# Keys and values by batch around the second batch's transposes, and the second heads of the first chunk half a granule later

## The reference

```
x = x + fake_quant(layernorm(x)) @ fake_quant(ctx)          # ctx: 2 x 2048 x 2048
h = layernorm(x)
q = h @ Wq                     # 2048 x 2048, 32 heads of 64
k, v = split(h @ Wkv)          # 2048 x 128: one key and one value head for all
p = softmax(causal(q k^T / 8 + alibi))
x = x + (p v) @ Wo             # 2048 x 2048
x = x + layernorm(x) @ dequant4(qweight, qzeros, scales) + bias
```

## Time and profile before

| | |
|---|---|
| median of 3 runs | 400.56 us (400.42 to 400.67) |
| profiled execution | 400.76 us |
| its span, first to last instruction | 398.9 us |
| granted TensorE clock, mean | 0.983 |
| PE busy | 353.4 us, 89% of the span |
| DVE busy | 328.7 us, 82% |
| ACT busy | 221.5 us, 56% |
| POOL busy | 29.7 us, 7% |
| DMA | 77.37 MB, mean 194 GB/s |

### The profile page before, as it was taken

The page is one execution under the profiler, slowest core; times in us unless marked ns, Lnnn a source line. Parts: engine busy times, 40 slices in busy tenths (PEclk is TensorE's granted clock), DMA queues, the critical chain, the costliest instruction groups (busy, mean ns, idle before and its releaser), DMA issues.

```text
span 398.9 us, 5679 instructions
## 1 busy us (share of the span) xinstructions
PE 353.4 (89%) x2321; PEld 262.9 (66%) x2326; DVE 328.7 (82%) x333; ACT 221.5 (56%) x316; POOL 29.7 (7%) x69
## 2 busy tenths in 40 slices
PE   0076867788799998999999999999999999999996
PEld 0022222325688786878877888888888788888884
DVE  1689889886877898785989968898988999999924
ACT  1788988998524873655855680743824923333100
POOL 6000000006590000000002000000000000000000
PEclk9999986999999999999999999999999999999999
DMA  8999999999063476496448733876000020000006
GB/s 327 426 429 434 428 422 432 430 395 379 6 218 128 182 194 197 140 214 209 159 159 248 218 108 115 305 273 257 3 0 1 0 107 0 2 0 0 2 0 210
DMA packets 21958, 77.37 MB, mean 194 GB/s; under 512 B 1354, under 2 KB 1402, under 8 KB 18810
## 3 DMA queue, kind: packets, MB, share of 16 engines
q1 hardware_dynamic: 21924, 77.01, 52.9%
q10 hardware_dynamic: 8, 0.00, 0.0%
HBM read 74.91 MB, written 2.10 MB: 193 GB/s over the span
## 4 chain that ended last, share of the span: by engine, by line
PE 69%; DMA 13%; DVE 9%; ACT 6%; issue 2%; ACTq 0%
PE bank L1186 21%; PE bank L1049 12%; PE bank L1050 12%; PE bank L1051 12%; DMA ctx_more<-in_ctx 12%; ACT q L462 5%; PE bank L1062 2%; PE bank L1131 2%; PE bank L1150 2%; DVE w_lo L652 2%; PE bank L1072 2%; DMA prm_row<-in_L_xattn_x_zp 1%; PE bank L1042 1%; DVE stats L622 1%; ACT a L467 1%
## 5 line engine op out<-in xcount | busy, mean ns | idle before, releaser
L486 ACT ACTIVATE w_hi<-raw 128x2048 fp32r<-128x2048 f32 x29 | 55.2, 1912 | 44.6 <-DMA raw<-in_L_attn_Wo 23.0
L652 DVE TENSOR_TENSOR w_lo<-raw,w_hi 128x2048 fp32r<-128x2048 f32 x27 | 62.4, 2321 | 13.2 <-ACT w_hi L486 13.2
L1186 PE MATMUL bank<-w_hi,hd 128*128 128x512 f32 x208 | 53.1, 391 | 0.1
L1010 PE MATMUL bank<-q,at 128*128 128x512 bf16 x123 | 38.0, 436 | 15.9 <-DVE q L708 14.7
L1186 PEld LDWEIGHTS bank<-w_hi,hd 128*128 128x128 f32 x208 | 38.8, 188 | 8.4 <-issue 0.5
L708 DVE TENSOR_SCALAR q<-q 128x2048 bf16<-128x2048 uint8 x32 | 38.4, 1218 | 4.9 <-PE bank L1017 3.0
L1049 PE MATMUL bank<-w_hi,hd 128*128 128x512 f32 x104 | 40.7, 391 | 0.0
L1050 PE MATMUL bank<-w_lo,hd 128*128 128x512 f32 x104 | 40.5, 389 | 0.0
L1051 PE MATMUL bank<-w_hi,hd 128*128 128x512 f32 x104 | 40.5, 389 | 0.0
L1049 PE MATMUL bank<-w_hi,xt 128*128 128x512 f32 x96 | 38.9, 405 | 0.0
L1050 PE MATMUL bank<-w_lo,xt 128*128 128x512 f32 x96 | 37.5, 390 | 0.0
(11 more groups left out here) (160 smaller groups left out, 618.0 us busy)
## 6 DMA issues: line engine op xcount, KB each, us to landing
raw<-in_ctx SPq DMA_DIRECT2D x8, 2048.0 KB, 15.4
raw<-in_L_attn_Wq SPq DMA_DIRECT2D x16, 1024.0 KB, 5.5
ctx_more<-in_ctx SPq DMA_DIRECT2D x7, 2048.0 KB, 16.2
raw<-in_L_attn_Wo SPq DMA_DIRECT2D x13, 1024.0 KB, 5.2
raw_fifth<-in_L_attn_Wo SPq DMA_DIRECT2D x3, 1024.0 KB, 5.1
resid<-in_x SPq DMA_DIRECT2D x2, 1024.0 KB, 12.7
ctx_more<-in_ctx SPq DMA_DIRECT2D x2, 1024.0 KB, 15.4
scale<-in_L_ffn_scales SPq DMA_DIRECT2D x16, 128.0 KB, 6.4
```

What stands on the lines that cost most here:

```text
L486: nc.scalar.activation(hi_slots[s], raw_slots[s], ACT.Copy).then_inc(w_hi_set, 1)
L652: nc.vector.tensor_tensor(lo_slots[s], raw_slots[s], hi_slots[s].bitcast(F32), ALU.subtract).then_inc(w_lo_set, 1)
L1010: mm(bank[:, 4 * b + n, :], at[:, k, b * P:(b + 1) * P], q16[:, i % 2, n * CH:(n + 1) * CH], start=start, stop=False)
L1186: return mm(bank[:, 4 * b + n, :], left[:, j, b * P:(b + 1) * P], right[slot_of(W_F + j)][:, n * CH:(n + 1) * CH], start=part == 0 and j = ...
```

## The change

On ACT the high part of the key and value weight is made ahead of `upper(1, g)`. On PE `keys_values` is replaced by `kv_by_upper(b)` (16 matmuls of 256 columns: both parts of x of one batch, with the high part of the weight) and `kv_by_lower()` (16 of 256 columns: high part of x of both batches, with the low part). `kv_by_upper(0)` stands right behind `transposes(1)`, the other two where `keys_values` stood. `q_by_lower(1, 0)` moves from behind the transposes to ahead of them. In the first turn of the loop (n = 1) `attend(ub)` moves behind `q_granule(w + 3, 1)`; in the others it stays.

```diff
             sqrt_of(3)
-            for g in range(4):
-                upper(1, g)
             act.wait_ge(wkv_loaded, 16)
             act.wait_ge(at_done, B)
             nc.scalar.activation(kv_hi_t, kv_raw[:], ACT.Copy).then_inc(kv_hi_set, 1)
+            for g in range(4):
+                upper(1, g)
...
-            def keys_values():
-
+            def kv_by_upper(b):
+
+                pe.wait_ge(kv_hi_set, 1)
+                pe.wait_ge(lo_out, 4 * (b + 1))
+                pe.wait_ge(resid1, B * NCH)
+                m = slice(b * P, (b + 1) * P)
+                for k in range(KT):
+                    mm(bank[:, KV_BANK, :].rearrange("p (x m) -> p x m", x=2)[:, :, m], kv_hi_t[:, k * P:(k + 1) * P],
+                       xt[:, :, k, m], start=b == 0 and k == 0, stop=False)
+
+            def kv_by_lower():
                 pe.wait_ge(kv_lo_set, 1)
-                pe.wait_ge(lo_out, 8)
-                pe.wait_ge(resid1, B * NCH)
                 for k in range(KT):
-                    c = slice(k * P, (k + 1) * P)
-                    if k > 0:
-                        mm(bank[:, KV_BANK, 0:B * P], kv_lo_t[:, c], xt_hi[:, k, :], start=False, stop=False)
-                    ins = mm(bank[:, KV_BANK, :], kv_hi_t[:, c], xt[:, :, k, :], start=k == 0, stop=k == KT - 1)
-                    if k == 0:
-                        mm(bank[:, KV_BANK, 0:B * P], kv_lo_t[:, c], xt_hi[:, k, :], start=False, stop=False)
+                    ins = mm(bank[:, KV_BANK, 0:B * P], kv_lo_t[:, k * P:(k + 1) * P], xt_hi[:, k, :],
+                             start=False, stop=k == KT - 1)
                 ins.then_inc(kv_done, 1)
...
             q_by_upper(3, 0)
+            q_by_lower(1, 0)
             transposes(1)
-            q_by_lower(1, 0)
+            kv_by_upper(0)
             for w in range(2):
                 q_by_upper(w, 1)
                 q_by_lower(w, 1)
...
             q_by_upper(3, 1)
-            keys_values()
+            kv_by_upper(1)
+            kv_by_lower()
             q_by_lower(3, 0)
...
                 q_granule(w + 3, 0)
-                attend(ub)
+                if n >= 2:
+                    attend(ub)
                 q_granule(w + 3, 1)
+                if n == 1:
+                    attend(ub)
```

## The result

| | before | changed |
|---|---|---|
| median | 400.51 us (400.42 to 400.67) | 397.31 us (397.11 to 397.71) |
| ratio | | 0.9921, 95% interval 0.9908 to 0.9933 |
| profiled execution | 400.76 us, span 398.9 | 397.71 us, span 395.9 |
| the changed kernel once more, beside its variants | 400.56 us | 397.56 us (397.15 to 397.65) |

The change is worth 3.2 us in the first comparison and 3.0 in the second. The forecast was 397.3, from a sum of 3.4. The profiled execution is the longest of its four.

A forecast was written before the change was run, and what follows sets the result against it. From about 93 us the kernel was taken as one long PE stream. Gains of 1.96 us (keys and values) and 1.48 (`attend(1)`) sum to 3.44, giving 397.3 us; forecast's own range 396.9 to 397.8, 8-in-10 range 396.7 to 399.0.

The forecast's parts named there:

- The three holes: PE idle before the second batch's transposes (1.34 us), behind `q_by_lower(1, 0)` (0.96) and before `attend(1)` (1.48): together 3.78 us.
- The lower product ahead of the transposes: `q_by_lower(1, 0)` runs from 103.2 to 104.1, shrinking the hole to about 0.5 us; by itself it gains nothing.
- The price of the narrow matmul: Keys and values: a 256-column matmul with its own load takes 0.115 us, at most 0.126; gain 1.96 us.
- ACT's copy: High part of the key and value weights, made ahead of `upper(1, g)`: ends at 104.4, 0.9 us early, costs nothing.
- Passed on at `kv_out`: DVE ends `kv_out` at about 124.6, half a microsecond before `value_rows` needs it, so the 1.96 us gain carries on.
- The third edit: First chunk: `attend(1)` goes behind `q_granule(7, 1)`, so PE no longer waits for `heads_lo(0)`; gain 1.48 us.
- the room at `scores(2)`: `heads_lo(1)` and `q_blocks(2)` end at 156.4, PE reaches `scores(2)` at 157.2: 0.8 us to spare.
- The loads did not bind in a long run: Denies a rival: weight loads and narrow matmuls go in turn, 0.31 us each, 5.6 us slower, 406.4; chance 0.04.
- The second rival: `heads_lo(1)` or `q_blocks(2)` is over 0.8 us later, so `scores(2)` takes over the wait: 398.8; chance 0.08.
- The front: Edits up to keys and values; rival: something keeps `kv_out` or `scores(0)` in place, only 1.48 gained, 399.3; chance 0.07.
- POOL's low part: Input of `q_by_lower(1, 0)`, said done at 102.45; rival: ready only at 106.4, transposes delayed, 400.1; chance 0.05.

The follow-up runs named there:

- the front alone: The changed kernel with `attend(1)` put back in front of `q_granule(7, 1)`, against the kernel before: 398.79 us, ratio 0.9954.
- the third edit alone: The kernel before with only `attend(1)` moved behind `q_granule(7, 1)`: 399.05 us, ratio 0.9964.

## Why the prediction was right, point by point

- *What bounds the kernel.* Right. The three holes were all that the change could reach, and closing them moved the end of the kernel by what they held, less the 0.44 us left of the first, the 0.12 us that 48 narrow matmuls take more than the mixed ones did (5.76 against 5.64), and the new wait.
- *The lower product ahead of the transposes.* Right: it ran at 103.09, left 0.44 us of the hole (0.5 was said), moved nothing behind it, and is worth nothing alone. The four long executions of it alone were not foreseen.
- *The price of the narrow matmul.* The one mis-sized term. I took 0.115 us from two neighbouring distances and gave 0.126 as the upper end. The long runs have 0.120 (16 in 1.91 us). So 32 x 0.120 = 3.83 us stay on the path and the gain is 1.81 in place of 1.96; the trace shows 1.77, the front alone measured 1.8.
- *ACT's copy.* Right: done at 104.33 (104.4 was said) and free of cost. With the copy in its old place PE waits 2.59 us.
- *Passed on at `kv_out`.* Right, with room of 0.7 us in place of 0.5; DVE's queue did become the limit there, as worked out, without mattering.
- *The third edit.* Right: 1.6 us by itself, the room at `scores(2)` 0.9 us in place of 0.8.
- *What was not seen.* "As long as the other engines keep feeding it" covered the wait at `attend(5)`, 0.2 to 0.3 us. In the trace of before that attention had no wait, but I had looked at its room in no row; it was 1.2 us, less than the landing of one load differs over the traces (9.8 to 11.3 us). That the first median fell on the forecast to 0.01 us is luck. The sum gave 397.2 from the median of before and 397.4 from its profiled execution, and I took the middle. The new wait (0.2 to 0.3 us) and the narrow matmuls (0.15) took something off, the third edit gave 0.1 more than its hole, and the second measurement is 397.56. All of this is well within the range.
- *The rivals.* The loads did not bind in a long run. The second rival's mechanism exists, and begins between 12 and 24 matmuls of lateness. The front paid in full, alone too (1.8 us). POOL's low part was not late (PE used it at 103.09).
- *The rule of the Trainium skill.* TensorE: Matmul & The Clock Gate, "The mechanism": that a weight load overlaps a running matmul only if its row group differs. Here 48 full-height loads, each of 0.19 us, stand in runs of 16 matmuls at 0.120 us apiece. The measurement decides: in this form they overlap, in a long run too, which fits the page's other statement, on loads into the background buffer. No run here shows which buffer they go to.

## What to carry to other kernels

An edit that is worth nothing alone can pay next to another: `q_by_lower(1, 0)` ahead of the transposes gains nothing by itself and 0.5 to 0.8 us with `kv_by_upper(0)` behind them. So first put work that is ready earlier into the hole in front, then fill the place that it leaves with work from further back, and check the engine that feeds that work for its own idle time. When a wait is dodged by moving the waiting step later, add up the steps that hang on it against the time until the next reader: here 0.9 us were left after 12 matmuls (2.7 us), and 12 more opened a hole of 2 us. A wait that is not there in one trace can have little room: read the room, not only the wait. Before moving a load, look at what is in flight just ahead of it too: in this kernel sixteen loads issued behind another one made the first land later.

## What the runs showed of the hardware

- A matmul of 256 columns with a weight load of its own costs 0.120 us in a long run, whether its moving operand is two pieces of 128 columns (line 1100) or one of 256 (line 1106); one of 512 costs 0.227.
- Holes in PE's stream can cost more than their length. After holes of 2.59 and 2.04 us the granted clock was near half for a while (0.52 over 3.5 us, 0.68 over 4 us), and 1.6 us were lost on top. Both kernels have executions shorter by about 1.5 us too, none of them traced. After the holes of 1.34, 1.48 and 1.53 us of the profiled kernels, and after the one of 1.89 us in the trace of the lower product alone, the clock stayed at 1.00. That the four longest executions of that kernel (1.5 us) are the same thing is likely by their size, but no trace was taken of one; the mean granted clock of the four (0.977, 0.978, and twice 0.982, against 0.981 to 0.987 in the other eight) does not settle it.
- The length of one hole does not decide whether the clock falls. In the trace of the changed kernel PE has holes of 1.67, 1.37, 1.67, 1.15 and 1.40 us between 58 and 71 us, with 1.2 to 1.4 us of work between them, and from 70 to 76 us the granted clock is 0.50. In the trace of the third edit alone it is 0.50 from 74 to 76 us, behind a hole of 2.35 us that ends at 72.78.
- Sixteen loads of 128 KB (each a row of scales copied to 16 partitions), issued behind one of 1 MB, moved its landing to 17.7 us, in both traces of such a kernel; in the others it is 14.1 or 14.2. From 99 to 102 us the DMA engines then were busy throughout and moved 175 GB/s; from 93 to 99 us of the changed kernel, busy throughout with other loads, they moved 399.
